# A convolution that builds each symmetric product once, with the MoE weights split a phase earlier and the last layer's first batch group taken batch by batch

## The chip, the cores and the metric

The kernel runs on one core of one Trainium2 chip. The metric is the device time of one execution in microseconds (us), inputs in HBM and output in HBM. The core's engines are TensorE (PE: matmuls, with PEld for its weight loads), VectorE (DVE), ScalarE (ACT), GpSimd (POOL) and SyncE (SP, which here only issues DMAs). Each has its own instruction stream; semaphores order them.

## What is computed

`x` is 16 batches x 128 tokens x 256 features. Four layers follow one another, each added to the residual `x`:

```python
# 1: gated long convolution. k = v = context, q = layernorm(x); 16 heads of 8 features
kv  = einsum('bhil,bhjl->bijhl', k, v)        # 8x8 products per head, channel and position
out = causal_conv(kv, ssm_kernel) + kv * D    # along l (256), by head
out = einsum('bijhl,bhil->bjhl', out, q)
# 2: MoE on layernorm(x): 16 routed experts (top 4 of the 2 best groups of 4) and a shared one
out = sum_e weight_e * (silu(x@gate_e) * (x@up_e)) @ down_e + swiglu(x, shared)
# 3: attention over features, per batch: softmax_d(q.T@k/16) applied to v = context
# 4: FFN of width 896 with LoRA experts, top 2 of 8 by softmax; silu(x1)*x3, twice
```

Here `l`, the 256 positions of the convolution, is the feature axis of `x`; the heads are cut from the token axis. Since `k = v`, `kv[i, j] = kv[j, i]`.

## The kernel before

`build` runs three phases one after the other: `first_phase` (convolution, the MoE's layernorm, router logits; 0 to 134.8 us), `moe_phase` (shared expert and routing to about 187, then the routed pairs to 351) and `tail_phase` (attention and the LoRA FFN). Each phase writes its engines' streams by hand; the order of the calls in each `@block` is the order on the engine. PE works in fp32 (two passes, shown as two matmul records) or, for the large products, in fp32r with each operand split in a high part `_hi` (a rounding copy) and a low part `_lo` (the rest) and three products, hi*hi, lo*hi and hi*lo.

**Convolution.** `CONV_ORDER` has 32 steps `(h, c)`: chunk `c` of 8 batches, head `h`. In step n POOL multiplies the 8x8 products of both halves of positions (L304, two instructions of 128x512) into one of 3 `kv` slots; PE multiplies them by the head's Toeplitz matrix (L408 to L410, three fp32 matmuls of 512 columns) into one of 2 pairs of PSUM banks; DVE multiplies by `q_t` (L545, twice 128x512) and sums over i (L554, twice) in place of `q_t`. From step 18 on, every third step also has one pair of tiles of the first chunk brought back: PE transposes it, DVE adds it to `x_sb` and takes statistics (`BACK_AT`, L501 to L514), POOL finds `rstd` (`RSTD_AT`, L251 to L257), ACT normalizes (L317), PE turns it, ACT copies it to `x_t` and casts to `x_hi` (L349, L352), POOL subtracts `x_lo` (L275). The second chunk's four pairs do the same behind the last step, with `x_lo` on DVE (L520).

**MoE weights.** 18 blocks of 128x768 are split. The first 8 go through a stage of 4 slots: ACT casts (L333), POOL subtracts (`weights_low(k)`, L269) at steps n = 2, 6, 10, ... ahead of the step's own products. The other 10 are split during the shared expert ("late"): ACT casts (L889) and writes the negative of the high part (L892), POOL adds the weight to it by an accumulating DMA (L962).

**Shared expert and routing.** 8 shared steps m. PE does gate and up (L583), ACT the silu (L872), DVE the product (`shared_product`, L1059), ACT the high part (L878), POOL the low part (L958), PE the down product (fp32r, `shared_down`); after each second step DVE adds two banks to `x_sb` (`add_to_x`, L1066, 2 x 128x512). Between these DVE finds the routing: top experts, ranks, slots, then one-hot tables for 4 blocks, `lane_hot` (L1101) and `tile_hot` (L1105, then times the token numbers, L1110), which PE turns into the list `slot_token` (L1119). POOL's gathers of the routed rows (L972) wait for that list. SP issues four loads of the last layer's weights (`lora_stage_early`, L723) when the table is done.

**Tail.** The routed rows are gathered back (L1657, 4 per batch). `attention_group` works on groups of 2 batches; group 0 runs alone ahead of the FFN: `add_routed` (L1755 to L1764), rstd on POOL (L605 to L609), `normalize` (L1772), scores on PE (L1459), `tops` (L1779), the exponentials on ACT (L1589), `scale_context` (L1786, L1793), `attention_out` (L1469), then the router (L1800 to L1853), the masks (L1610) and the first masked LoRA inputs `mix` (L1866), with which the FFN's steady work starts.

## Time and profile before

| | us |
|---|---|
| median of 3 runs | 859.78 |
| lowest, highest | 859.76, 860.88 |
| the profiled execution | 855.01 |
| its span | 853.3 |
| mean granted TensorE clock | 0.948 of full speed |
| busy: PE, DVE, POOL, ACT | 729.5, 549.2, 464.0, 328.3 |

The profile is of one execution. Its own time is 855.01 us, of which 853.3 lie between the first and the last instruction; it is 4.8 us under the median. A row of the timeline is one instruction, or a run of like ones: start, duration, engine, line, operation, output and inputs, count, and in brackets the idle time of the engine ahead of it with what ended that.

### The profile page before, as it was taken

To read this page: it belongs to the slowest core of one execution; us is meant where nothing else is said; L and a number is where in the kernel's file an instruction comes from. 1 tells how busy PE (TensorE), PEld (TensorE's weight loads), DVE (VectorE), ACT (ScalarE), POOL (GpSimd) and SP (SyncE) were. 2 spreads that over 40 slices of the span, in tenths; PEclk is the share of its full clock that TensorE was granted. 3 is DMA by queue.
4 is the path that set the end of the run, shared out by engine and by line. 5 is a ranking of instruction groups with operands and counts; after the bars stand their busy time and mean duration, and the time that the engine had idled before them with its cause. 6 is when DMAs were issued, how large, how long until landed. Compare 5 with 4: busy or idle time off the path is not lost.

```text
span 853.3 us, 14835 instructions
## 1 busy us (share of the span) xinstructions
PE 729.5 (85%) x5249; PEld 656.3 (77%) x5249; DVE 549.2 (64%) x1328; ACT 328.3 (38%) x680; POOL 464.0 (54%) x549
## 2 busy tenths in 40 slices
PE   4899989836778778238789999999999999999996
PEld 2344557736777778127789999999999999999996
DVE  4799977993445555348676767667666767654533
ACT  2221246612444445314454344444453343434321
POOL 4898963546455442336436636556475564543432
PEclk9899997967999999768899999999999999999999
DMA  8410014874555556342410201102011010000000
GB/s 257 152 38 12 26 37 122 186 157 160 147 152 144 139 146 123 106 139 77 127 35 25 65 1 57 32 13 63 13 32 57 1 50 27 1 14 1 2 13 13
DMA packets 42583, 63.16 MB, mean 74 GB/s; under 512 B 7152, under 2 KB 31760, under 8 KB 42512
## 3 DMA queue, kind: packets, MB, share of 16 engines
q1 hardware_dynamic: 34064, 38.71, 13.9%
q0 software_dynamic: 8352, 23.47, 12.3%
q8 instruction: 44, 0.72, 0.4%
q14 instruction: 27, 0.22, 0.1%
q10 hardware_dynamic: 96, 0.04, 0.0%
HBM read 47.37 MB, written 14.84 MB: 73 GB/s over the span
## 4 chain that ended last, share of the span: by engine, by line
PE 41%; DVE 6%; issue 4%; ACT 4%; POOL 3%; DMA 0%; POOLq 0%; ACTq 0%; DVEq 0%
PE bank L1387 15%; PE bank L1372 8%; PE bank L1419 6%; PE bank L1433 3%; PE bank L1405 3%; PE bank L1469 2%; DVE hid_lo L1883 2%; PE bank L1446 1%; ACT att_weights L1589 1%; POOL rows_back L1657 1%; DVE att_scaled L1793 1%; DVE am_lo L1872 1%; ACT am_hi L1574 1%; PE bank L1507 1%; ACT lora_w_hi L1550 1%
## 5 line engine op out<-in xcount | busy, mean ns | idle before, releaser
L1675 POOL TENSOR_TENSOR hid<-hid,rw_sb 128x256 f32<-128x256 f32 x112 | 90.7, 810 | 154.6 <-DVE hid L1877 154.4
L1387 PE MATMUL bank<-am_hi,lora_w_hi 128*128 128x256 f32 x448 | 126.9, 283 | 3.4 <-DVE am_lo L1872 3.4
L1877 DVE TENSOR_TENSOR hid<-hid,bank 128x256 f32<-128x256 f32 x112 | 46.7, 418 | 124.9 <-ACT hid L1557 124.2
L1387 PE MATMUL bank<-am_hi,lora_w_lo 128*128 128x256 f32 x448 | 126.7, 283 | 0.0
L1387 PE MATMUL bank<-am_lo,lora_w_hi 128*128 128x256 f32 x448 | 126.6, 283 | 0.0
L972 POOL DMA_INDIRECT rows_in<-y_scratch,slot_token x80 | 76.7, 958 | 76.5 <-DVE row_w L1173 44.6
L1557 ACT ACTIVATE hid<-bank 128x256 f32<-128x256 f32 x112 | 42.4, 385 | 183.3 <-PE bank L1387 170.7
L1387 PEld LDWEIGHTS bank<-am_hi,lora_w_hi 128*128 128x128 f32 x448 | 85.3, 190 | 3.6 <-POOL am_lo L1686 3.6
L1657 POOL DMA_INDIRECT rows_back<-slots_scratch,comb_idx x64 | 66.5, 1039 | 37.7 <-POOLq L666 22.2
L1387 PEld LDWEIGHTS bank<-am_hi,lora_w_lo 128*128 128x128 f32 x448 | 85.4, 191 | 0.0
L1387 PEld LDWEIGHTS bank<-am_lo,lora_w_hi 128*128 128x128 f32 x448 | 85.3, 190 | 0.0
L1883 DVE TENSOR_TENSOR hid_lo<-hid,hid_hi 128x256 fp32r<-128x256 f32 x112 | 71.2, 656 | 18.6 <-ACT hid_hi L1563 13.5
L1372 PE MATMUL bank<-lora_x_hi,lora_w_hi 128*128 128x256 f32 x224 | 67.8, 303 | 4.2 <-DVE lora_w_lo L1748 4.2
L304 POOL TENSOR_TENSOR kv<-ctx_t 128x512 f32<-128x512 f32 x64 | 64.7, 1042 | 2.8 <-PE bank L410 2.8
L1419 PE MATMUL bank<-hid_hi,lora_w_hi 128*128 128x256 f32 x224 | 62.9, 281 | 0.7 <-DVE hid_lo L1883 0.7
L1372 PE MATMUL bank<-lora_x_lo,lora_w_hi 128*128 128x256 f32 x224 | 63.2, 282 | 0.0
L1372 PE MATMUL bank<-lora_x_hi,lora_w_lo 128*128 128x256 f32 x224 | 63.1, 282 | 0.0
L1419 PE MATMUL bank<-hid_lo,lora_w_hi 128*128 128x256 f32 x224 | 62.6, 279 | 0.0
L1419 PE MATMUL bank<-hid_hi,lora_w_lo 128*128 128x256 f32 x224 | 62.5, 279 | 0.0
L1194 DVE SCALAR_TENSOR_TENSOR routed_h<-routed_silu,slot_w,bank 128x128 f32<-128x128 f32 x80 | 24.2, 344 | 50.2 <-issue 32.8
L545 DVE TENSOR_TENSOR prod<-bank,q_t 128x512 f32<-128x512 f32 x64 | 41.0, 682 | 17.4 <-PE bank L410 16.6
L848 PE MATMUL bank<-moe_w_hi,ht_hi 128*128 x80 | 24.4, 305 | 30.3 <-DVE ht_lo L1167 30.3
(259 smaller groups left out, 2245.6 us busy)
## 6 DMA issues: line engine op xcount, KB each, us to landing
slots_scratch<-y_out SPq DMA_DIRECT2D x40, 256.0 KB
lora_stage_early<-in_lora_weights SPq DMA_DIRECT2D x16, 384.0 KB, 3.2
...
```

The costliest lines, as they stand in the source:

```text
L304: last = nc.gpsimd.tensor_tensor(kv[:, n % KV_SLOTS, m, :].rearrange("p (b j i) -> p b j i", j=HEAD_DIM, i=HEAD_DIM), feat.unsqueeze(2).br ...
L545: nc.vector.tensor_tensor(prod[:, m, :].rearrange("p (b j i) -> p b j i", j=HEAD_DIM, i=HEAD_DIM), conv_banks[2 * (n % CONV_SETS) + m][:, ...
L972: nc.gpsimd.indirect_dma_start(out=rows_in[:, i % ROW_SLOTS, :], out_offset=None, in_=y_dram[:, :], in_offset=bass.IndirectOffsetOnAxis(ap ...
L1372: nc.tensor.matmul(x_banks[F % 2][:, w * GT:(w + 1) * GT], wp, xp, start=(w == 0 and c == 0 and k == 0), stop=False, skip_group_check=True)
L1387: last = nc.tensor.matmul(x_banks[F % 2][:, w * GT:(w + 1) * GT], wp, ap, start=False, stop=(half == 1 and k == 2), skip_group_check=True)
L1405: last = nc.tensor.matmul(a_banks[w][:, half * GT:(half + 1) * GT], wp, xp, start=(c == 0 and k == 0), stop=(c == HALVES - 1 and k == 2))
L1419: last = nc.tensor.matmul(term_banks[which][:, half * GT:(half + 1) * GT], wp, hp, start=(n == 0 and half == 0 and j == 0), stop=(n == FB ...
L1557: nc.scalar.activation(f[:, F % 2, k, :], x_banks[F % 2][:, 0:GT], ACT.Silu).then_inc(silu_done, 1)
L1657: nc.gpsimd.indirect_dma_start(out=rows_back[:, t % ROW_TILES, k * DIM:(k + 1) * DIM], out_offset=None, in_=slots_dram[:, :], in_offset=ba ...
L1675: nc.gpsimd.tensor_tensor(f[:, F % 2, k, :], f[:, F % 2, k, :], rw_sb[:, F // FB % 2, k, :], ALU.mult)\
L1877: nc.vector.tensor_tensor(f[:, F % 2, k, :], f[:, F % 2, k, :], x_banks[F % 2][:, GT:2 * GT], ALU.mult)\
L1883: nc.vector.tensor_tensor(hid_lo[:, F % 2, which, :], f[:, F % 2, 1 - which, :], hid_hi[:, F % 2, which, :].bitcast(FP32), ALU.subtract).t ...
```

## The change

- Convolution steps with odd n build 48 of the 64 products: 4x4 (low, low), which is enough for its quarter, and 8x4 (all, high); POOL has two instructions (128x16x16 and 128x16x32, these are 256 and 512 elements), PE 384 columns for each of the three matmuls, DVE three products (256, 256, 512 elements) and one sum of 1024. Even steps do all 64 with one instruction of 1024 on POOL and one product and one sum of 1024 on DVE. `prod` has one buffer for both.
- All 18 weight blocks are split in the first phase, by the method of the late ones: ACT casts and negates, POOL issues the accumulating DMA (`LOWS_AT`). There are 2 stage slots. The ACT order is new; `toeplitz(2)` is loaded ahead of the stage; row 3 of the queries is normalized on ACT.
- End of the first phase: `x_t` has 3 slots, and for the second chunk DVE does both the cast and the subtraction (`x_parts`).
- Shared down product from the unsplit fp32 rows: 4 fp32 matmuls per step, no high and low parts. `add_to_x` is replaced by two ACT copies (`shared_rows`) and a POOL accumulating DMA from SBUF to SBUF (`add_rows`), 4 times. The token-number products of blocks 0 to 2 are on ACT (`token_numbers`); `LANE_ORDER` is 0, 1, 2, 3.
- The four early LoRA loads stand one each ahead of the first four stores of routed rows.
- In the tail, group 0's chain is in the order of its batches: rstd, normalize, top, inverse, scale by batch, the gathers of batch 0 in one step and of batch 1 in the next two; `base(1)` follows `spread_picks`, and `mix` waits for its own mask only.

```diff
-SPLIT_EARLY = HEADS // 2
-STAGES, LATE_STAGES = 4, 2
+STAGES = 2
-LANE_ORDER = (0, 2, 1, 3)
+LANE_ORDER = (0, 1, 2, 3)
+HALF_HEAD = HEAD_DIM // 2
+OWN, KV_COLS = HALF_HEAD * HALF_HEAD, HALF_HEAD * (HALF_HEAD + HEAD_DIM)
+LOWS_AT = {5 + 2 * k if k < 3 else 11 + 5 * (k - 3) // 4: k for k in range(FBLOCKS)}
...
             def weights_low(k):
-                pool.wait_ge(hi_split, k + 1)
-                nc.gpsimd.tensor_tensor(w_lo[:, W_ORDER[k], :], stage[:, k % STAGES, :],
-                                        w_hi[:, W_ORDER[k], :].bitcast(FP32), ALU.subtract).then_inc(lo_split, 1)
+                pool.wait_ge(hi_split, 2 * k + 2)
+                nc.gpsimd.dma_start(w_lo[:, W_ORDER[k], :], a["moe_weights"][W_ORDER[k]], accum_op=ALU.add)\
+                  .then_inc(lo_split if k else first_low, 16)
...
-                if n % 4 == 2:
-                    weights_low(n // 4)
+                if n in LOWS_AT:
+                    weights_low(LOWS_AT[n])
...
+                low, high = feat[:, :, 0:HALF_HEAD], feat[:, :, HALF_HEAD:HEAD_DIM]
+                for first, rows, columns in (((0, low, low), (OWN, feat, high)) if distinct(n) else ((0, feat, feat),)):
...
             def weights_high(k):
                 act.wait_ge(staged[k % STAGES], 16 * (k // STAGES + 1))
                 nc.scalar.copy(w_hi[:, W_ORDER[k], :], stage[:, k % STAGES, :]).then_inc(hi_split, 1)
+                act.wait_ge(hi_split, 2 * k + 1)
+                nc.scalar.mul(w_lo[:, W_ORDER[k], :], w_hi[:, W_ORDER[k], :].bitcast(FP32), -1.0).then_inc(hi_split, 1)
...
+            query_copy(0)
+            query_rows(3)
+            for p in range(1, FIRST_HALF):
                 query_copy(p)
...
+            for k in range(3, FBLOCKS):
+                weights_high(k)
...
+                cols = slice(0, KV_COLS if distinct(n) else ALL_COLS)
...
+                if distinct(n):
+                    parts = ((low, low, out[:, :, 0:OWN].rearrange("p n (j i) -> p n j i", i=HALF_HEAD)),
+                             (low, high, out[:, :, OWN:2 * OWN].rearrange("p n (j i) -> p n j i", i=HALF_HEAD)),
+                             (high, everything, out[:, :, OWN:KV_COLS].rearrange("p n (i j) -> p n i j", j=HALF_HEAD)))
+                for j, i, y_ji in parts:
+                    shape = [P, width, j.stop - j.start, i.stop - i.start]
+                    last = nc.vector.tensor_tensor(prod[:, :, j, i], y_ji,
+                                                   query[:, :, i].unsqueeze(2).broadcast_to(shape), ALU.mult)
+                last.then_inc(prod_ready, 1)
...
-            def x_low(e):
+            def x_parts(e):
+                dve.wait_ge(xt_copied, e + 1)
+                x, hi, lo = x_t[:, e % X_SLOTS, :, :], token_cols(x_hi, 2 * P * e, 2 * P), token_cols(x_lo, 2 * P * e, 2 * P)
+                nc.vector.tensor_copy(hi, x).then_inc(hi_done, 1)
                 dve.wait_ge(hi_done, e + 1)
+                nc.vector.tensor_tensor(lo, x, hi.bitcast(FP32), ALU.subtract).then_inc(lo_done, 1)
...
-            for k in range(STAGE_SLOTS):
-                sp.dma_start(lora_stage[:, k, :], lora_unit(a, k)).then_inc(lora_staged, 16)
             for q in range(ROUTED_PAIRS):
                 sp.wait_ge(y_copied, q + 1)
+                if q < STAGE_SLOTS:
+                    sp.dma_start(lora_stage[:, q, :], lora_unit(a, q)).then_inc(lora_staged, 16)
...
                 for t in range(GROUP_T // P):
-                    rows = slice(t * P, (t + 1) * P)
-                    w = w_hi[:, n, 2 * DIM:3 * DIM], w_lo[:, n, 2 * DIM:3 * DIM]
...
+                    last = nc.tensor.matmul(out_banks[t // 2][:, (t % 2) * DIM:(t % 2 + 1) * DIM],
+                                            act[:, m % 2, t * P:(t + 1) * P], down_w[:, n, :],
+                                            start=(first and t % 2 == 0), stop=last_one, skip_group_check=True)
...
+            def shared_rows(g):
+                act_eng.wait_ge(down_done, SHARED_BLOCKS * (g + 1))
...
+                for o in range(2):
+                    nc.scalar.copy(shared_out[:, g % 2, 2 * o:2 * o + 2, :],
+                                   out_banks[o][:, :].rearrange("p (t d) -> p t d", t=2)).then_inc(out_copied, 1)
...
+            def add_rows(g):
+                pool.wait_ge(out_copied, 2 * (g + 1))
+                nc.gpsimd.dma_start(x_sb[:, 4 * g:4 * g + 4, :], shared_out[:, g % 2, :, :], accum_op=ALU.add)\
+                  .then_inc(x_added[g % 2], 16)
...
+            def token_numbers(block):
+                act_eng.wait_ge(tile_hit, block + 1)
+                for u in range(block * HOT_TILES, (block + 1) * HOT_TILES):
+                    rows = slice(u * TOP_EXPERTS, (u + 1) * TOP_EXPERTS)
+                    nc.scalar.activation(tile_hot[:, rows, :], tile_hot[:, rows, :], ACT.Copy,
+                                         scale=token_ids[:, u:u + 1]).then_inc(hot_ready, 1)
...
-            for t in range(TG):
-                add_routed(t)
+            add_routed(0)
+            normalize(0)
+            add_routed(1)
+            find_top(0)
+            normalize(1)
+            find_inverse(0)
+            scale_context(0)
+            find_top(1)
+            find_inverse(1)
+            scale_context(1)
```

The order of the instructions on POOL around step 2 of the convolution (`kv` are the products, `moe_w_lo` the low parts of the weights), before:

```order
L304 TENSOR_TENSOR kv<-ctx_t 128x512 x4
L269 TENSOR_TENSOR moe_w_lo<-early_stage,moe_w_hi 128x768
L304 TENSOR_TENSOR kv<-ctx_t 128x512 x8
L251 TENSOR_SCALAR rstd<-meanvar 128x4
L252 TENSOR_SCALAR shift<-meanvar 128x4
```

And after:

```order
L325 TENSOR_TENSOR kv<-ctx_t 128x1024
L325 TENSOR_TENSOR kv<-ctx_t 128x16x16
L325 TENSOR_TENSOR kv<-ctx_t 128x16x32
L325 TENSOR_TENSOR kv<-ctx_t 128x1024
L325 TENSOR_TENSOR kv<-ctx_t 128x16x16
L325 TENSOR_TENSOR kv<-ctx_t 128x16x32
L325 TENSOR_TENSOR kv<-ctx_t 128x1024
L290 DMA moe_w_lo<-in_moe_weights 128x768
```

The first low part of the weights moved from ahead of step 2 to ahead of step 5, and is a DMA.

On DVE at the end of the routing (`moe_act` is a shared product; `lane_hot` and `tile_hot` are the one-hot tables of a block; `reached` begins the tile table), before:

```order
L1101 TENSOR_TENSOR lane_hot<-lanes,lane_of 128x2048
L1059 TENSOR_TENSOR moe_act<-moe_silu,bank 128x512
L1066 TENSOR_TENSOR x_sb<-x_sb,bank 128x512 x2
L1105 TENSOR_TENSOR tile_hot<-tile_ids,tile_of 128x1280
L1110 TENSOR_SCALAR tile_hot<-tile_hot,token_ids 128x320 x4
L1101 TENSOR_TENSOR lane_hot<-lanes,lane_of 128x2048
L1105 TENSOR_TENSOR tile_hot<-tile_ids,tile_of 128x1280
L1110 TENSOR_SCALAR tile_hot<-tile_hot,token_ids 128x320 x4
L1101 TENSOR_TENSOR lane_hot<-lanes,lane_of 128x2048
```

And after:

```order
L1133 TENSOR_TENSOR lane_hot<-lanes,lane_of 128x2048
L1098 TENSOR_TENSOR moe_act<-moe_silu,psum 128x512
L1137 TENSOR_TENSOR tile_hot<-tile_ids,tile_of 128x1280 x2
L1133 TENSOR_TENSOR lane_hot<-lanes,lane_of 128x2048
L1137 TENSOR_TENSOR tile_hot<-tile_ids,tile_of 128x1280
L1144 TENSOR_SCALAR tile_hot<-tile_hot,token_ids 128x320 x4
L1133 TENSOR_TENSOR lane_hot<-lanes,lane_of 128x2048
```

The additions to `x_sb` and all but the last block's products with the token numbers left DVE's stream.

On DVE at the start of the tail (`rows_back` are the gathered rows of a batch), before:

```order
L1764 BN_AGGR meanvar<-stats 128x2
L1772 TENSOR_SCALAR att_y<-x_sb,meanvar,rstd 128x256 x2
L1779 TENSOR_REDUCE att_minus_top<-bank6 128x2
L1779 TENSOR_REDUCE att_minus_top<-bank7 128x2
L1786 RECIPROCAL att_inverse<-att_total 128x2 x2
L1793 TENSOR_SCALAR att_scaled<-ctx_ring,att_inverse 128x128 x4
```

And after:

```order
L1806 TENSOR_SCALAR att_y<-x_sb,meanvar,rstd 128x256
L1790 TENSOR_TENSOR rows_back<-rows_back 128x512
L1794 TENSOR_TENSOR x_sb<-x_sb,rows_back 128x256 x2
L1797 BN_STATS stats<-x_sb 128x6
L1799 BN_AGGR meanvar<-stats 128x2
L1811 TENSOR_REDUCE att_minus_top<-psum 128x2
L1806 TENSOR_SCALAR att_y<-x_sb,meanvar,rstd 128x256
L1816 RECIPROCAL att_inverse<-att_total 128x2
L1824 TENSOR_SCALAR att_scaled<-ctx_ring,att_inverse 128x128 x2
```

Batch 0's rows are normalized ahead of the addition of batch 1's routed rows, and its maximum, inverse and scaling stand beside batch 1's.

## Rows read from the trace of the kernel before

**Rows 1.** Timeline of DVE, steady convolution steps; start, duration, instruction, idle before
```profile
50.95 1.29 DVE L545 TENSOR_TENSOR prod<-bank,q_t 128x512 f32<-128x512 f32 x2 [0.98 <-PE bank L410]
53.52 1.29 DVE L545 TENSOR_TENSOR prod<-bank,q_t 128x512 f32<-128x512 f32 x2
...
77.76 1.25 DVE L545 TENSOR_TENSOR prod<-bank,q_t 128x512 f32<-128x512 f32 x2
...
80.12 1.28 DVE L545 TENSOR_TENSOR prod<-bank,q_t 128x512 f32<-128x512 f32 x2
```

**Rows 2.** Timeline of POOL, the wait ahead of step 2
```profile
21.10 1.81 POOL L269 TENSOR_TENSOR moe_w_lo<-early_stage,moe_w_hi 128x768 fp32r<-128x768 f32 x1 [6.00 <-ACT moe_w_hi L333]
```

**Rows 3.** Timeline of DVE, first product and the product behind the wait
```profile
18.93 1.29 DVE L545 TENSOR_TENSOR prod<-bank,q_t 128x512 f32<-128x512 f32 x2 [4.73 <-PE bank L410]
...
30.50 0.69 DVE L545 TENSOR_TENSOR prod<-bank,q_t 128x512 f32<-128x512 f32 x1 [4.99 <-PE bank L410]
```

**Rows 4.** Table by stretch: length; busy us of PE, PEld, DVE, ACT, POOL; clock, DMA share, GB/s
```profile
28.00:30.00 2.00, 2.00 (x3) 0.70 (x3) 0.00 (x0) 0.29 (x1) 0.89 (x1) 0.50 0.36 132
...
77.00:118.00 41.00, 38.35 (x133) 19.86 (x131) 36.03 (x71) 10.67 (x18) 35.51 (x43) 1.00 0.08 26
...
176.00:187.00 11.00, 5.10 (x60) 4.42 (x59) 10.93 (x16) 0.00 (x0) 0.86 (x1) 0.66 0.70 153
```

**Rows 5.** Timeline of DVE, short rows of 4, and the end of the routing
```profile
143.86 0.63 DVE L1024 TENSOR_TENSOR choice<-choice,g_mask 128x64 f32<-128x64 f32 x4
...
185.53 1.49 DVE L1116 TENSOR_TENSOR reached<-tile_nums,tile_end 128x1280 f32<-128x1280 f32 x1
187.06 0.24 DVE L1119 CAST slot_token<-bank 128x80 int32<-128x80 f32 x1
```

**Rows 6.** Timeline of DVE, a step with a pair brought back, and the last sums
```profile
73.94 0.68 DVE L501 TENSOR_TENSOR x_sb<-x_sb,bank 128x512 f32<-128x512 f32 x1
74.56 1.29 DVE L545 TENSOR_TENSOR prod<-bank,q_t 128x512 f32<-128x512 f32 x2
...
117.19 1.27 DVE L554 TENSOR_REDUCE q_t<-prod 128x64 f32<-128x512 f32 x2
```

**Rows 7.** Groups by line (busy us, mean ns, idle before), and all issues of L962 (ns, min/median/max)
```profile
L304 POOL TENSOR_TENSOR kv<-ctx_t 128x512 f32<-128x512 f32 x64 | 64.7, 1042 | 2.8 <-PE bank L410 2.8
...
L962 POOL DMA_DIRECT2D moe_w_lo<-in_moe_weights x10: 863/880/1142, 143.2 to 176.0; - x10
```

**Rows 8.** Timeline of ACT, a split by cast and negation; first normalized rows of the end
```profile
79.46 1.09 ACT L317 ACTIVATE y<-x_sb,shift,rstd 128x256 f32<-128x256 f32 x2 [17.96 <-POOL shift L257]
...
158.07 0.82 ACT L889 CAST moe_w_hi<-rows_in 128x768 fp32r<-128x768 f32 x1
158.91 0.85 ACT L892 ACTIVATE moe_w_lo<-moe_w_hi 128x768 fp32r<-128x768 f32 x1
```

**Rows 9.** Timeline of PE, the last logits of the first phase
```profile
131.02 3.43 PE L446 MATMUL bank<-moe_gate,moe_x_t 128*128 128x16 f32 x16
```

**Rows 10.** Timeline of DVE, routing tables beside the shared expert
```profile
167.70 0.94 DVE L1110 TENSOR_SCALAR tile_hot<-tile_hot,token_ids 128x320 f16<-128x320 f16 x4
...
171.36 1.28 DVE L1066 TENSOR_TENSOR x_sb<-x_sb,bank 128x512 f32<-128x512 f32 x2
172.55 2.93 DVE L1105 TENSOR_TENSOR tile_hot<-tile_ids,tile_of 128x1280 f16<-128x1280 f16 x1
...
178.58 1.48 DVE L1105 TENSOR_TENSOR tile_hot<-tile_ids,tile_of 128x1280 f16<-128x1280 f16 x1
```

**Rows 11.** Timeline of DVE: first rows of the routed loop, then group 0 in the tail
```profile
193.23 0.19 DVE L1173 TENSOR_TENSOR row_w<-rows_in,is_expert 128x32 f32<-128x32 f32 x1 [1.19 <-DMA rows_in<-y_scratch,slot_token]
...
364.30 0.69 DVE L1755 TENSOR_TENSOR rows_back<-rows_back 128x512 f32<-128x512 f32 x1 [2.72 <-DMA rows_back<-slots_scratch,comb_idx]
...
378.67 0.69 DVE L1800 TENSOR_TENSOR x_sb<-x_sb,bank 128x512 f32<-128x512 f32 x1 [3.68 <-PE bank L1469]
```

**Rows 12.** Table by stretch, start of the routed loop
```profile
192.00:197.00 5.00, 1.11 (x4) 0.71 (x4) 1.02 (x4) 0.58 (x1) 3.78 (x5) 0.50 0.96 366
```

359 lines of the change are left out of this document (172 added, 187 removed).

## The prediction

> **What bounds the kernel now.** I read the shares by engine first: TensorE (PE) is busy 729.5 of 853.3 us and carries the end of the chain. But the diff leaves the FFN's steady work and the routed loop as they are, so the question is which engine's wait ends last in each of the four places that it does touch. Those are read from the timelines.
>
> In the steady convolution the products on VectorE (DVE) start at 50.95, 53.52 and so on, 2.57 us apart, with an idle 0.98 in one of them that PE ends: PE is the bound, its three fp32 matmuls take 0.857 each. Where DVE has fallen behind it runs 2.36 per step [rows 1]. GpSimd (POOL) needs 2 x 1.04 = 2.1 [rows 7]. The three engines are nearly equal, so a gain on PE alone is small. One stop stands out: POOL waits 6.00 us ahead of step 2 for a high part of the weights [rows 2], DVE's product behind it comes 4.99 late [rows 3], and TensorE's granted clock is 0.50, its lower level of 1.2 GHz, while it recovers [rows 4]. From step 18 on no engine is full: in the 41 us from 77 to 118 PE is busy 38.35, DVE 36.03, POOL 35.51 [rows 4]; they wait for one another. While the routing is made DVE is the bound, busy 10.93 of 11.00 us before the list of slots at 187.06 [rows 4, 5]. The routed loop begins when the first gather lands, at 193.23, and the tail's start is a chain of group 0 through all engines [rows 11].
>
> **Convolution steps.** PE: even steps keep 3 x 0.857 = 2.57; odd ones have 384 of 512 columns, 1.93; mean 2.25, 0.32 less. POOL: an odd step has 768 elements instead of 1024, about 0.5 less than 2.1, if a row of 4 costs no more than its elements. DVE gets dearer: now product waits for sum and sum for product in one buffer. Rate: 1280 elements take 1.49 [rows 5], that is 0.15 + N/960; so 1024 take 1.22, with a gap of 0.03 twice 2.50 for an even step; an odd one 2 x 0.33 + 0.72 + 1.25 = 2.62, mean 2.56. That short rows are no dearer is read from four instructions with rows of 4 that take 0.63 together [rows 5]. So DVE replaces PE as the bound at 2.56, where it was 2.57: **the symmetric steps themselves give nothing in the first half** and take away what slack DVE had. Without any gain or with all of PE's they would be between 2.36 and 2.62.
>
> **The stop at step 2.** It goes, because nothing stands ahead of the products of steps 0 to 4. The first product was at 18.93 [rows 3] and is put at 18.0, since POOL's kv is not earlier but DVE has one row of queries less. Step 18's was at 74.56 [rows 6]. After: 18.0 + 18 x 2.56 + two rounds of statistics for queries that hid in the stop, 3.5, = 67.6. Gain 7.0. If conv steps take 2.62, 5.9; if the start stays, 0.9 less.
>
> **Steps 18 to 31.** Before, 74.56 to 118.46 (the sums at 117.19 take 1.27 [rows 6]), 43.9. DVE after: 14 x 2.56 plus four pairs brought back at 1.46 (73.94 to 77.76 is 3.82, less 2.36 [rows 1, 6]) = 41.7. POOL has here 3.5 less for products, and 9 issues of 0.88 [rows 7] in place of four subtractions of 1.81 [rows 2]: 0.7 more; busy about 33, no bound. Gain 1.9, between 0 and 3. Convolution together **8.9, range 6 to 10**.
>
> What the split adds to ScalarE (ACT): 18 units of 0.82 + 0.85 [rows 8] = 30.1 where 8 casts stood, in streams that were idle (17.96 ahead of its row at 79.46 [rows 8]). A pair of units is a cycle of about 5.2 with two stage slots (load 3.9 behind the first cast, by the page's median landing of such a load), so the 15 units behind the queries run from about 41 to 74 or 79. The first normalized rows are wanted at 76.5 then. A lateness of up to 3 us is possible and is partly caught by the pairs' spacing of three steps; I take 0, and 3 for the range.
>
> **End of the first phase.** From the last sum to the barrier it is a chain over four pairs. ACT's cast, 0.62 a pair, leaves it, the third slot of `x_t` takes the wait for logits away; DVE's extra cast is shorter than ACT's pace. PE's last logits took 3.43 at a low clock [rows 9] and stay. Four casts are 2.5, of which the last one was not on the path of the logits: gain **2, range 1.5 to 2.5**.
>
> **Routing.** What leaves DVE ahead of the slot list: three `add_to_x` at 1.20 (the row of 1.28 with its overlap) and three times four products with the token numbers at 0.86 (0.94) [rows 10], 6.2. And what POOL's subtractions did to DVE beside them: `tile_hot` took 2.93 where the same one took 1.48 [rows 10], another one 2.24; a few short ones of the top search went from 0.22 to 1.22 in the same way; in all 4.6, which go with the subtractions. That makes 10.8. The Trainium skill (SBUF — State Buffer, "SBUF: two separate sides") says that a DVE instruction with two SBUF inputs and a POOL one that reads SBUF lock each other out for the whole instruction; the row of 2.93 agrees, and without that rule the sum would be 6.2. PE is then the next late one: its fp32 down product is 4 matmuls of 0.43 = 1.7 instead of 12 of 0.117 = 1.4, and gate and up stay at 2.8 per step, at a clock that is low at first; two waits of DVE for it cost about 2.5 to 3.3. Gain at the list **7.5, range 6 to 10**: 179.6 instead of 187.06. Nothing of it waits on the list's path for the new copies on ACT (four times 1.1) or the additions by DMA, except that the last addition's DMA (512 KB, issued near 175) stands on POOL's queue ahead of the first gather: about 8 us from issue to landing, so until 183, as the gather lands 183 or later too. Cost 0, at most 2.
>
> **Start of the routed loop.** The first gather lands 5.65 after POOL's start at 187.58; DMA engines were busy 0.96 with 366 GB/s in 192 to 197 [rows 12], mostly the four LoRA loads of 384 KB. They now follow the first four pairs. Landing of a gather in the quiet tail takes 1.8 from its issue; here 3.2 and 4.4. Gain **2.5, range 1 to 3**. The loads are behind `y_copied`, needed first in the tail, 150 us later; SP queues only stores there, late by 0.1 each.
>
> **Tail start.** The chain before: batch 1's rows 364.30, att 378.67 [rows 11], then router and `mix` at 394.7. By batch, batch 0's normalization, scores (half of a cold 3.7) and exponentials stand in the wait for batch 1's rows; behind 364.3 there remain one batch's 2.1 of additions and statistics, rstd 1.4, one normalization, half the scores, one maximum, two exponentials, two scalings and half of `attention_out`: att at about 375.0, 3.7 earlier. A further 0.7 comes from the mask wait. Gain **4.4, range 3 to 5**. The FFN behind it is full on PE and moves with it.
>
> **Sum.** 8.9 + 2 + 7.5 + 2.5 + 4.4 = 25.3. The profiled execution of 855.01 becomes 829.7; it lies 4.8 under the median of the runs shown, 859.78, which I keep: **834.5**.
>
> **Rivals.** *First, ACT's weight chain is late.* If the accumulating DMA holds a slot longer or loads crowd with the second context load, the end rows come 3 to 6 us late and a part of the end chain with them: 834.5 + 4 = 838.5. For it: two slots instead of four; POOL waited for such a split 6.00 once [rows 2]. Against: ACT's 17.96 idle [rows 8].
> *Second, DVE is a bound that I priced too low*: extra gaps in odd steps, three dependent instructions, or slots that no longer overlap. At 2.8 per step, + 0.24 x 32 = 7.7, 842. It speaks for it that three engines lie within 15% [rows 1, 7].
> *Third, slower than before: rows of four are dear.* Place: the three DVE products of an odd step write and read 256 rows of 4 per partition. Each ns of a row's fixed cost is 0.256 us per odd step, 4.1 us in 16; it decides at 25.3/4.1 = 6.2 ns a row. At 10 ns the time is 875. Against it: 16 rows of 4 take 0.16 us [rows 5], 2 ns a row by the constants above.
> *Fourth, the change doesn't do what it says*: PE now idles in each step, and the granted clock falls to 1.2 GHz in the convolution, as it is 0.50 behind the stop and 0.66 at 176 to 187 [rows 4]. A step would take PE 4.5 instead of 2.56. That for half of the steps is + 31, 865. Against: at 38.35 busy of 41 it is 1.00 [rows 4].
> *Fifth, a better one*: the cover is looser and DVE reaches 2.45 per step, and all 10 of the routing: 834.5 - 3.5 - 2.5 = 828.5. The Trainium skill (same page and section) warns of the opposite, that DMA descriptors made by POOL wait while DVE holds the shared port in its fast modes; the longest of ten issues here was 1.14 against 0.88 [rows 7], so it would add at most 0.3 x 18 = 5 to a queue that has room.
>
> **How the numbers follow.** Forecast 0.52 (832 to 837), first rival 0.14, second 0.14, better one 0.12, slower one 0.03, clock 0.02 (865: slower too), no measurable change 0.03 by several of them together. Leaving out the last 0.08 and the far end of the others, the range is 827 to 843. The chance of faster by more than 0.2% (1.7 us, about what a measurement of this kernel can tell) is 0.93, same 0.02, slower 0.05.
>
> **What the profile of the changed kernel would show.** No wait of POOL over 1 us in the first 40 us, and clock 1.00 there; step 18 near 67.6; DVE steps of 2.50 and 2.62 in turn with PE waiting for DVE; last sum near 109.6, barrier near 124; slot list 44.9 behind the barrier (before 52.3); first routed row 3.5 behind the first gather's issue; tail's `mix` at 38 instead of 43.0 behind the loop's end. It would be wrong by a step that takes over 2.7, by ACT's units that end behind 80, or if the routing wait moved to PE and kept more than 4 us.

## The result: 1.5% faster, half of what was forecast

The changed kernel takes 848.12 us (median of 4 runs, 846.94 to 850.94), the kernel before 860.33 in the same job: ratio 0.9853, 95% interval 0.9823 to 0.9884, 12.2 us less. The forecast was 834.5 with a range of 827 to 843; the sign was right, the size and the range were wrong. The profiled execution of the changed kernel took 847.37, with a span of 845.6 and a mean granted clock of 0.945; it lies 7.6 under the profiled one of before. That one lay 4.8 under its median, this one 0.75.

Read by landmarks of the two profiles (start of a row; the last line is the last addition to `x_sb`):

| stretch | before | changed | difference | forecast |
|---|---|---|---|---|
| start to step 18's product | 74.56 | 71.21 | -3.4 | -7.0 |
| to the last sum's end | 43.9 | 51.6 | **+7.7** | -1.9 |
| to the router's scores | 16.3 | 16.5 | +0.2 | -2 |
| to the slot list | 52.3 | 45.8 | -6.5 | -7.5 |
| to the first routed row | 6.2 | 4.8 | -1.4 | -2.5 |
| routed loop, to the tail's first row | 158.4 | 162.2 | **+3.8** | 0 |
| tail to the first `mix` | 43.0 | 37.8 | -5.2 | -4.4 |
| to the last addition | 455.4 | 452.5 | **-2.9** | 0 |

The stop ahead of step 2 is gone, as forecast, and the steady steps of the convolution take 2.65 us on average: 2.58 from the start of an even step to the next one, 2.71 from an odd one. In this timeline of DVE of the changed kernel the columns are start, duration, instruction and the idle time before it, as in [rows 1]:

```profile
37.88 1.23 DVE L586 TENSOR_TENSOR prod<-psum,q_t 128x1024 f32<-128x1024 f32 x1
39.14 1.22 DVE L593 TENSOR_REDUCE q_t<-prod 128x128 f32<-128x1024 f32 x1
40.46 1.35 DVE L586 TENSOR_TENSOR prod<-psum,q_t 128x256 f32<-128x256 f32 x3
41.85 1.22 DVE L593 TENSOR_REDUCE q_t<-prod 128x128 f32<-128x1024 f32 x1
43.17 1.23 DVE L586 TENSOR_TENSOR prod<-psum,q_t 128x1024 f32<-128x1024 f32 x1
...
94.41 1.23 DVE L586 TENSOR_TENSOR prod<-psum,q_t 128x1024 f32<-128x1024 f32 x1 [11.12 <-PE psum L443]
```

The last row is the loss: a new stop of 11.12 us ahead of step 22. It is followed through the engines. PE, same kernel:

```profile
77.18 0.81 PE L443 MATMUL psum<-kv,toeplitz 128*128 128x384 f32 x2
89.36 1.11 PE L468 MATMUL psum<-ident,y 128*128 128x128 f32 x4 [11.38 <-ACT y L339]
90.27 1.91 PE L441 MATMUL psum<-kv,toeplitz 128*128 128x512 f32 x2
```

PE stands in front of the first turn of the end rows (`turn_rows(0)`, L468, in step 22 ahead of the step's own product) and waits for ACT's rows `y`; behind the wait its first product takes 1.91 instead of 1.02, at a granted clock of 0.50 (89.4 to 92 us), the lower level. ACT, same kernel, has the first of the 15 splits behind the queries, the last one and the rows:

```profile
43.58 0.84 ACT L355 CAST moe_w_hi<-stage 128x768 fp32r<-128x768 f32 x1
...
86.62 0.83 ACT L355 CAST moe_w_hi<-stage 128x768 fp32r<-128x768 f32 x1 [1.35 <-DMA stage<-in_moe_weights]
87.48 0.84 ACT L357 ACTIVATE moe_w_lo<-moe_w_hi 128x768 fp32r<-128x768 f32 x1
88.23 1.08 ACT L339 ACTIVATE y<-x_sb,shift,rstd 128x256 f32<-128x256 f32 x2
```

15 units from 43.58 to 88.32 are 2.98 each; the same row of before came at 79.46 [rows 8]. The reason for the length is in the idle brackets: ACT waits for the stage's load, 19.4 us in all of these 44.7. The page gives those loads 5.3 us to landing:

```profile
stage<-in_moe_weights SPq DMA_DIRECT2D x18, 384.0 KB, 5.3
moe_w_lo<-in_moe_weights POOLq DMA_DIRECT2D x18, 384.0 KB, 6.1
```

The theory I took to the chip: the end rows are queued behind 18 splits on ACT, PE meets their turn in order and stops, and that alone is most of what is missing. The rival: the splits' transfers and issues fill the second part anyway, and the wait only moves.

### The profile page after: what moved, and what is told of

Its sections match the earlier page's. It is cut to its first block, busy times and chain, and to the rows that moved or that the text cites. A ratio compares the mean times of both kernels' runs of the same rounds, so it can differ in the third digit from the quotient of the medians.

```text
span 845.6 us, 14731 instructions
## 1 busy us (share of the span) xinstructions
PE 725.4 (86%) x5217; PEld 660.0 (78%) x5217; DVE 542.3 (64%) x1278; ACT 339.8 (40%) x698; POOL 442.6 (52%) x532
## 4 chain that ended last, share of the span: by engine, by line
PE 48%; DVE 3%; POOL 3%; issue 2%; ACT 2%; POOLq 0%; DVEq 0%
PE psum L1417 18%; PE psum L1402 9%; PE psum L1449 8%; PE psum L1463 4%; PE psum L1435 3%; PE psum L1489 1%; PE psum L1476 1%; POOL rows_back L1688 1%; PE psum L1499 1%; PE psum L1537 1%; DVE lora_w_lo L1783 1%; PE psum L1517 1%; ACT lora_w_hi L1581 1%; PE psum L1507 0%; PE psum L1530 0%
## 5 line engine op out<-in xcount | busy, mean ns | idle before, releaser
L1417 PE MATMUL psum<-am_hi,lora_w_hi 128*128 128x256 f32 x448 | 128.0, 286 | 2.4 <-DVE am_lo L1903 2.1
L1417 PE MATMUL psum<-am_hi,lora_w_lo 128*128 128x256 f32 x448 | 127.8, 285 | 0.0
L1417 PE MATMUL psum<-am_lo,lora_w_hi 128*128 128x256 f32 x448 | 127.7, 285 | 0.0
L1417 PEld LDWEIGHTS psum<-am_hi,lora_w_hi 128*128 128x128 f32 x448 | 86.5, 193 | 3.0 <-POOL am_lo L1719 2.3
L1914 DVE TENSOR_TENSOR hid_lo<-hid,hid_hi 128x256 fp32r<-128x256 f32 x112 | 74.7, 688 | 19.4 <-ACT hid_hi L1594 14.5
L1417 PEld LDWEIGHTS psum<-am_lo,lora_w_hi 128*128 128x128 f32 x448 | 86.6, 193 | 0.0
L1417 PEld LDWEIGHTS psum<-am_hi,lora_w_lo 128*128 128x128 f32 x448 | 86.5, 193 | 0.0
L1402 PE MATMUL psum<-lora_x_hi,lora_w_hi 128*128 128x256 f32 x224 | 67.0, 299 | 6.1 <-DVE lora_w_lo L1783 6.1
L325 POOL TENSOR_TENSOR kv<-ctx_t 128x1024 f32<-128x1024 f32 (+2 forms) x48 | 64.6, 1517 | 5.1 <-PE psum L443 5.1
L1449 PE MATMUL psum<-hid_hi,lora_w_hi 128*128 128x256 f32 x224 | 62.9, 281 | 0.7 <-DVE hid_lo L1914 0.7
L1402 PE MATMUL psum<-lora_x_lo,lora_w_hi 128*128 128x256 f32 x224 | 62.6, 280 | 0.0
```

Source lines behind the costliest of these rows:

```text
L325: last = nc.gpsimd.tensor_tensor(kv[:, n % KV_SLOTS, :, first:first + shape[2] * shape[3]].rearrange("p n (i j) -> p n i j", j=shape[3]), ...
L1402: nc.tensor.matmul(x_banks[F % 2][:, w * GT:(w + 1) * GT], wp, xp, start=(w == 0 and c == 0 and k == 0), stop=False, skip_group_check=True)
L1417: last = nc.tensor.matmul(x_banks[F % 2][:, w * GT:(w + 1) * GT], wp, ap, start=False, stop=(half == 1 and k == 2), skip_group_check=True)
L1449: last = nc.tensor.matmul(term_banks[which][:, half * GT:(half + 1) * GT], wp, hp, start=(n == 0 and half == 0 and j == 0), stop=(n == FB ...
L1914: nc.vector.tensor_tensor(hid_lo[:, F % 2, which, :], f[:, F % 2, 1 - which, :], hid_hi[:, F % 2, which, :].bitcast(FP32), ALU.subtract).t ...
```

## Experiments

Four jobs of kernels (e, f, g, i), each timed beside the kernel before. Times of different jobs are compared through their ratios to it; "its partner" is the kernel that a run was edited from, e4_parts_behind_rstd for the runs f and g3. That kernel has 0.968 in job e and, repeated as i3, 0.971 in job i, so a difference of 0.003 between jobs is not told from none. Landmarks are of one profiled execution each.

| run | median us | ratio to before (95%) |
|---|---|---|
| e1_interleaved | 836.58 | 0.970 (0.965 to 0.976) |
| e2_no_stage_loads | 835.64 | 0.970 (0.966 to 0.974) |
| e3_no_symmetry | 840.43 | 0.975 (0.971 to 0.979) |
| e4_parts_behind_rstd | 835.52 | 0.968 (0.964 to 0.972) |
| f1_early_lora_loads | 837.01 | 0.971 (0.966 to 0.975) |
| f2_numbers_on_vector | 838.92 | 0.975 (0.971 to 0.978) |
| f3_group_by_pair | 837.06 | 0.973 (0.969 to 0.977) |
| f4_sum_in_halves | 834.85 | 0.971 (0.967 to 0.976) |
| g1_before_late_lora | 822.52 | 0.998 (0.996 to 1.000) |
| g2_before_new_tail | 812.89 | 0.988 (0.984 to 0.991) |
| g3_lows_two_later | 796.55 | 0.967 (0.964 to 0.971) |
| i1_changed_again | 846.76 | 0.983 (0.977 to 0.990) |
| i2_attention_by_group | 857.06 | 0.996 (0.993 to 0.999) |
| i3_repaired_again | 835.23 | 0.971 (0.965 to 0.977) |
| i4_both_repairs | 834.86 | 0.970 (0.965 to 0.976) |

### The order on ScalarE

```diff
-            for k in range(3, FBLOCKS):
+            for k in range(3, 14):
                 weights_high(k)
             for e in range(FIRST_HALF):
                 end_rows(e)
+                if 14 + 2 * e < FBLOCKS:
+                    weights_high(14 + 2 * e)
                 x_columns(e)
                 x_high(e)
+                if 15 + 2 * e < FBLOCKS:
+                    weights_high(15 + 2 * e)
```

> The changed kernel with one edit: on ScalarE the last four weight units stand between the first chunk's end rows instead of all ahead of them. My theory (end rows queued behind 18 splits stop TensorE at step 22, in order): TensorE's wait of 11.4 us ahead of the first turn of the end rows falls below 2, the last sum of the convolution comes at about 110 to 112 instead of 122.8, and the time falls from 848.1 by 10 to 12 us, to 836 to 838. Rival (the splits' DMAs or GpSimd's issues fill the second part, so that the wait only moves to GpSimd's low parts): the last sum stays behind 118 and the gain is under 4 us.

It measured 836.58, a ratio of 0.970 against 0.985 for the changed kernel. In the trace the last sum ends at 112.6 instead of 122.8, and this table of PE's waits from 70 to 115 us (in total, how often, longest) no longer has the end rows in it:

```profile
PE psum L445 <- POOL kv L325: 3.6, 4, 1.6
PE psum L460 <- DVE q_t L597: 2.1, 1, 2.1
PE psum L445 <- DVE prod L590: 0.2, 1, 0.2
```

ACT now has the rows at 75.28, between two splits:

```profile
74.37 0.84 ACT L357 ACTIVATE moe_w_lo<-moe_w_hi 128x768 fp32r<-128x768 f32 x1
75.28 1.09 ACT L339 ACTIVATE y<-x_sb,shift,rstd 128x256 f32<-128x256 f32 x2
78.92 0.83 ACT L355 CAST moe_w_hi<-stage 128x768 fp32r<-128x768 f32 x1 [2.54 <-DMA stage<-in_moe_weights]
```

So the splits had room in the second part, and the rival falls. The second run asks what makes the chain so long.

```diff
             for k in range(STAGES, FBLOCKS):
-                sp.wait_ge(hi_split, 2 * (k - STAGES) + 1)
-                load_stage(k)
+                pass
...
-                act.wait_ge(staged[k % STAGES], 16 * (k // STAGES + 1))
+                act.wait_ge(staged[k % STAGES], 16)
```

> The changed kernel without the stage loads of blocks 2 to 17: ScalarE splits what lies in the two slots, so the weights of the routed experts are wrong, and everything else is done. ScalarE's order is that of the changed kernel. If the chain of splits is bound by load and landing behind the two slots (2.98 us per unit measured, ScalarE's own part 1.67), it now ends near 70 instead of 88.3, the stop at step 22 vanishes and the time is 836 to 839. If ScalarE itself or its place behind the queries is the bound, the chain still ends behind 80 and at least half of the stop stays, 842 or more.

835.64. The edit also takes the traffic of these 16 loads away. With the order of the changed kernel, but nothing to wait for, the splits end at 67 and ACT then waits for GpSimd:

```profile
66.24 0.84 ACT L356 ACTIVATE moe_w_lo<-moe_w_hi 128x768 fp32r<-128x768 f32 x1
74.34 1.09 ACT L338 ACTIVATE y<-x_sb,shift,rstd 128x256 f32<-128x256 f32 x2 [7.26 <-POOL shift L277]
```

Either repair alone is enough: the stop is the product of a chain bound by its loads and of a queue order that put the urgent rows behind it. More stage slots, the plain remedy, were not tried.

### What the symmetric steps are worth

```diff
 def distinct(n):
-    return n % 2 == 1
+    return False
```

> As e1_interleaved, but all steps build all 64 products (one product and one sum of 1024 elements each on VectorE). My theory, that the symmetric steps give nothing because VectorE is the bound: an even step measured about 2.58 us, an odd one 2.71, so without symmetry TensorE takes over at 2.57 to 2.6 and the convolution is as long or up to 2 us shorter than in e1_interleaved. Rival (the 0.64 us less of TensorE and 0.5 of GpSimd per odd step is what makes room for the end work from step 18 on): 3 to 8 us longer than e1_interleaved.

840.43, 3.85 above its partner in the same job: the rival was nearer, at its lower end, though the two intervals overlap (0.971 to 0.979 and 0.965 to 0.976). Up to step 18 it is 1.1 behind (71.54 against 70.47, 0.85 of it already at the first product), from there 2.3 more (the sums end at 115.99 against 112.63). In these two traces 2.4 of the 3.4 are given back before the scores, 1.5 of them because the last logits ran at a clock of 1.00 here and of 0.50 there, as told below. So the symmetric steps are worth 3.4 us at the last sum, and what of it reaches the end isn't narrowed. With all products PE is busy 40.45 of the 42 us from 70 to 112; with 48 of them in odd steps it is busy 36.73 and DVE 39.26. These are the rows of e3_no_symmetry and of e1_interleaved in the table by stretch, columns as in [rows 4]:

```profile
70.00:112.00 42.00, 40.45 (x131) 20.14 (x130) 36.78 (x47) 19.34 (x29) 38.83 (x39) 1.00 0.68 154
```

```profile
70.00:112.00 42.00, 36.73 (x137) 20.63 (x136) 39.26 (x62) 20.19 (x30) 36.83 (x45) 1.00 0.65 145
```

From the first product to step 18 the two kernels are equal within 0.2 us (51.6 and 51.3), so there the symmetric steps give nothing, as forecast. From step 18 on the turns, transposes and logits share PE with the products and find room. My statement that symmetry gives nothing held for the first half alone.

### The end of the phase

```diff
+            dve.wait_ge(rstd_step, 3 * PAIRS_T)
             for e in range(FIRST_HALF, PAIRS_T):
                 x_parts(e)
```

> As e1_interleaved, and VectorE begins x_parts only when GpSimd has found all rstd of the end. In the changed kernel GpSimd's last four small instructions, beside VectorE's x_parts, took 2.5 us where their like took 1.4. My theory (the two lock each other out): the four take 1.4 again, the last end rows begin 1.1 us earlier, and the time is 0.5 to 1.5 us below e1_interleaved. Rival (the slowness is not from x_parts, or x_parts then are late themselves): no change or up to 1 us slower.

835.52 against 836.58, with intervals that overlap: the medians don't tell the two apart, the traces do. The changed kernel, GpSimd and VectorE at the last rstd:

```profile
130.30 0.32 POOL L272 TENSOR_SCALAR rstd<-meanvar 128x2 f32<-128x2 f32 x1 [0.18 <-DVE meanvar L547]
130.71 0.64 POOL L273 TENSOR_SCALAR shift<-meanvar 128x2 f32<-128x2 f32 x1
131.31 0.90 POOL L275 TENSOR_TENSOR rstd<-rstd,minus_half 128x2 f32<-128x2 f32 x1
132.29 0.66 POOL L278 TENSOR_TENSOR shift<-shift,rstd 128x2 f32<-128x2 f32 x1
```

```profile
130.13 0.41 DVE L553 CAST moe_x_hi<-moe_x_t 128x512 fp32r<-128x512 f32 x1
130.58 0.69 DVE L555 TENSOR_TENSOR moe_x_lo<-moe_x_t,moe_x_hi 128x512 fp32r<-128x512 f32 x1
131.75 0.43 DVE L553 CAST moe_x_hi<-moe_x_t 128x512 fp32r<-128x512 f32 x1 [0.48 <-ACT moe_x_t L373]
132.21 0.69 DVE L555 TENSOR_TENSOR moe_x_lo<-moe_x_t,moe_x_hi 128x512 fp32r<-128x512 f32 x1
```

And e4_parts_behind_rstd, the same four of GpSimd:

```profile
120.65 0.23 POOL L272 TENSOR_SCALAR rstd<-meanvar 128x2 f32<-128x2 f32 x1 [0.17 <-DVE meanvar L551]
120.96 0.22 POOL L273 TENSOR_SCALAR shift<-meanvar 128x2 f32<-128x2 f32 x1
121.13 0.71 POOL L275 TENSOR_TENSOR rstd<-rstd,minus_half 128x2 f32<-128x2 f32 x1
121.92 0.20 POOL L278 TENSOR_TENSOR shift<-shift,rstd 128x2 f32<-128x2 f32 x1
```

The four take 2.65 us from the first start to the last end in the changed kernel and 1.47 in e4_parts_behind_rstd. Each of the four slow ones ends 0.03 to 0.08 us behind the end of the VectorE instruction beside it: the 0.64 that began at 130.71 ends at 131.35, the subtraction at 131.27. The Trainium skill (SBUF — State Buffer, "SBUF: two separate sides") describes the shared port pair as held by one of the two for a whole instruction. These ends agree with it.

The stretch from the last sum to the scores is 16.7 in e1_interleaved and 14.2 here, but the lock is only half of that. The stretch ends with PE's last logits, sixteen matmul records. They begin 12.9 us behind the last sum in e1_interleaved and 11.6 here; in all six traces of changed kernels without the wait they begin at 12.0 to 12.9, in all eight with it at 11.2 to 11.7, before at 12.6. That difference, 1.1 us between the means, is what the wait gives. How long they then take follows the granted clock, 3.43 us at 0.50, 2.22 at 0.82 and 1.90 at 1.00:

```profile
135.57 3.43 PE L479 MATMUL psum<-moe_gate,moe_x_t 128*128 128x16 f32 x16
```

```profile
137.65 1.90 PE L479 MATMUL psum<-moe_gate,moe_x_t 128*128 128x16 f32 x16
```

The first row is of the changed kernel, the second of i1_changed_again, the same kernel in another execution, whose stretch is 14.3 without any repair. With the wait the stretch is 13.7 to 15.4 in eight traces. So the wait gives about 1 us, and the other 1.2 of e4's are the clock of that one execution.

### The routed loop and the LoRA loads

In every changed kernel of the first two jobs the loop took 161.0 to 163.9 us from the first row to the tail; before it took 158.4 in its one trace. ACT, changed kernel, among the first pairs:

```profile
199.77 0.58 ACT L948 CAST moe_xt_hi<-psum 128x512 fp32r<-128x512 f32 x1 [2.48 <-remote]
205.49 0.38 ACT L961 ACTIVATE routed_silu<-psum 128x256 f32<-128x256 f32 x1 [5.13 <-remote]
```

The matmuls of the second row's silu are done by the records at 199.4; "remote" is a releaser that the trace has no record of. Is it the moved loads?

```diff
+            for k in range(STAGE_SLOTS):
+                sp.dma_start(lora_stage[:, k, :], lora_unit(a, k)).then_inc(lora_staged, 16)
             for q in range(ROUTED_PAIRS):
                 sp.wait_ge(y_copied, q + 1)
-                if q < STAGE_SLOTS:
-                    sp.dma_start(lora_stage[:, q, :], lora_unit(a, q)).then_inc(lora_staged, 16)
```

> As e4_parts_behind_rstd (835.5 us), with the four LoRA loads back ahead of the routed loop. In the four kernels with the loads in the loop, the stretch from the first routed row to the tail takes 162.0 to 163.7 us, before it took 158.4, and the stretch from slot list to first row 4.8 instead of 6.2. If the moved loads cause the longer loop, it is 158.5 to 160 here and the time is 1 to 3 us lower; the first row lands 6 us behind the list again. If they do not (something else holds ScalarE at the third pair, for 5.1 us), the loop stays at 162 or more and the time is 1 to 2 us higher.

837.01. The first row lands 5.9 behind the list again and the fourth pair comes 19.7 behind it, as before (21.9 in its partner), but from first row to tail it is 162.0, unchanged, and the same hold of 5.13 us is there, one silu earlier. Not the loads. The opposite edit, alone on the kernel before:

> The kernel before with only the four LoRA loads moved behind the first routed pairs. In the profile of before the first routed row came 6.2 us behind the slot list and the fourth pair 19.7 behind it. My forecast gave this move 2.5 us. If the fourth pair is held by something else (in all changed kernels ScalarE stands still for about 5.1 us once among the first pairs, and the fourth pair comes 19.7 to 21.9 behind the list whenever the first row landed), the first row comes at 4.8 but the fourth pair not before 19.5, and the time is within 1 us of before. If the move pays, the fourth pair comes at 17 to 18 and the time is 2 to 3 us lower.

822.52 to 824.39, ratio 0.998 (0.9963 to 0.9997). In this job the kernel before took 824 us instead of 860, for a reason that isn't known. It has no trace of its own there; in the trace of g1_before_late_lora the 40 pairs take 112.9 us from the first to the last, 2.89 each, where the trace of before has 146.4 and 3.75. These 33.5 us are nearly all of the difference. The loop has no wait of ACT for "remote":

```profile
230.68 0.38 ACT L919 ACTIVATE routed_silu<-bank 128x256 f32<-128x256 f32 x1 [0.34 <-PE bank L825]
231.61 0.37 ACT L898 CAST ht_hi<-bank 128x256 fp32r<-128x256 f32 x1 [0.55 <-PE bank L834]
232.05 0.59 ACT L906 CAST moe_act_hi<-bank 128x512 fp32r<-128x512 f32 x1
232.53 0.59 ACT L912 COPY y_out<-bank 128x512 f32<-128x512 f32 x1
233.47 0.39 ACT L919 ACTIVATE routed_silu<-bank 128x256 f32<-128x256 f32 x1 [0.34 <-PE bank L825]
```

The fourth pair came 14.3 behind the list, less than both cases of the expectation; with the loads ahead of the loop, in g2_before_new_tail of the same job, it came 17.9 behind. In this job the loads' price is 1.9 us by the medians, at most 3 by the interval.

### The tail

```diff
             add_routed(0)
-            normalize(0)
             add_routed(1)
-            find_top(0)
+            normalize(0)
             normalize(1)
-            find_inverse(0)
-            scale_context(0)
+            find_top(0)
             find_top(1)
+            find_inverse(0)
             find_inverse(1)
+            scale_context(0)
             scale_context(1)
```

> As e4_parts_behind_rstd, with VectorE's order of group 0 in the tail back to both batches at each stage. From the tail's first instruction to the first mix it is 37.8 to 38.9 us now, 43.0 before. If that order is what the tail gained by, it is 41 to 43 here and the time 3 to 5 us higher. Rival (the masks and the moved base product are what counts): under 40 and less than 2 us higher.

837.06, ratio 0.973 against 0.968 and 0.971, which doesn't tell it from its partner. The trace has 39.7 us to the first mix against 38.8: the order on VectorE alone is worth about 1, and the rival holds. The whole tail on the kernel before:

> The kernel before with the whole tail of the changed one. In the changed kernel the tail, from its first instruction to the last addition, is 8.1 us shorter than before, 5.2 of it ahead of the first mix. If the tail's edit makes all of it, the time is 6 to 8 us under before; if only the start is its doing, 4 to 5.

812.89, 11.5 under before by the medians; the ratio, 0.988 (0.984 to 0.991), allows 7 to 13, so it is above the lower case and perhaps above the upper. By landmarks, against the trace of g1_before_late_lora in the same job, 5.2 of it is ahead of the first mix and 6.1 behind it, in the FFN's steady work that I had called unchanged. The rows that show it are PE's waits from first mix to the end, kernel before and changed kernel:

```profile
PE bank L1469 <- DVE att_scaled L1793: 7.9, 7, 4.2
PE bank L1372 <- DVE lora_w_lo L1748: 4.2, 4, 1.2
```

```profile
PE psum L1402 <- DVE lora_w_lo L1783: 6.1, 5, 1.4
PE psum L1499 <- DVE att_scaled L1824: 3.6, 1, 3.6
```

The attention product waited 7 times, 7.9 us in all, now once for 3.6; the waits for `lora_w_lo` grew from 4.2 to 6.1. The last job takes that one edit back out of the changed kernel:

```diff
-                for k in range(TG):
-                    pe.wait_ge(exp_done, HALVES * (TG * G + k + 1))
-                    pe.wait_ge(scaled_done, HALVES * (TG * G + k + 1))
+                pe.wait_ge(exp_done, HALVES * TG * (G + 1))
+                pe.wait_ge(scaled_done, HALVES * TG * (G + 1))
+                for k in range(TG):
```

> The changed kernel, where TensorE's attention product again waits for both batches of its group before it begins. In the kernel before, that product waited for VectorE's scaled context in 7 of 8 groups, 7.9 to 8.7 us in all, 4.2 to 5.0 of it once; in the changed kernel once behind group 0, 3.6. If these waits by batch are the part of the tail's gain that I missed, six or seven groups lose 0.7 each again: the stretch from the first mix to the end grows by 3 to 5 us, and the time is 4 to 6 us above i1_changed_again. Rival (the moved weight units and the mask's wait did it): under 1.5 us.

857.06 against 846.76 for the changed kernel beside it: 10.3 us, of the 13.6 that the whole change gained in that job. The waits are back:

```profile
PE psum L1499 <- DVE att_scaled L1824: 8.1, 7, 4.4
```

By landmarks it is 1.7 ahead of the first mix and 4.4 behind it, 6.1 of the 6.9 that the two profiled executions differ by. The profiled execution of i1_changed_again took 851.14, 4.4 above its median (its routing has a wait of 2.52 for TensorE that no other trace has), so the traces can't place the rest of the 10.3. The wait of `attention_out`, which the diff changes for all eight groups, carries most of the tail's gain; its size is 6 by the traces and 10 by the medians, and I can't narrow it.

### VectorE and GpSimd in the repaired kernel

```diff
-            for block in range(HOT_BLOCKS - 1):
-                token_numbers(block)
```

(with the products back on VectorE for all blocks)

> As e4_parts_behind_rstd, with the products of the one-hot tables with the token numbers of blocks 0 to 2 back on VectorE. From scores to slot list the changed kernels take 45.8 us. If VectorE bounds that stretch alone, three groups of four at 0.86 come on top: 48.4, and the time is 2.6 us higher. If TensorE's shared steps bound it (4.46 us between two of them, VectorE waits of 0.5, 1.6 and 0.2 for it), part of it hides: 46.5 to 47.5, 1 to 2 us higher.

838.92, ratio 0.975 against 0.968 and 0.971. From scores to list it is 48.5 against 45.8, 2.7: VectorE bounds that stretch, and the sum's price of 0.86 a group was right. Two edits to its partner for the convolution:

> As e4_parts_behind_rstd, with VectorE's sum in two halves of 512 in each step and the product of an even step in two halves, so that an instruction seldom waits for the one right before it. If the waits between product and sum (spacing 1.26 and 1.33 of instructions of 1.22) are what makes VectorE the bound of the steps, a pair of steps takes 4.9 to 5.1 instead of 5.30, the last sum comes 3 to 5 us earlier and the time is 831 to 833. Rival (the extra instructions cost as much as the waits, or GpSimd is the next bound at once): within 1 us of e4_parts_behind_rstd.

834.85, ratio 0.971: no gain, the rival. Its last sum comes at 115.2, no earlier than the 114.8 of f1_early_lora_loads in the same job, whose convolution is the partner's. The instructions did get denser, but from step 7 on VectorE waits 0.34 for TensorE in each pair of steps, and two steps take 5.4. This timeline of TensorE in f4_sum_in_halves shows why:

```profile
42.83 1.02 PE L447 MATMUL psum<-kv,toeplitz 128*128 128x512 f32 x2
43.69 1.04 PE L428 MATMUL psum<-ident,y 128*128 128x128 f32 x8
44.56 0.81 PE L445 MATMUL psum<-kv,toeplitz 128*128 128x384 f32 x2
...
49.87 0.91 PE L445 MATMUL psum<-kv,toeplitz 128*128 128x384 f32 x2 [0.64 <-POOL kv L325]
```

TensorE is busy without a gap over steps 7 to 10 (10.70 of 10.70 us from 38.5 on): the products of two steps, 4.50, and the turns of the queries, 0.87, are 5.37. Behind them it waits for GpSimd's products. Where VectorE stops being the bound, TensorE or GpSimd is the next at once.

```diff
-LOWS_AT = {5 + 2 * k if k < 3 else 11 + 5 * (k - 3) // 4: k for k in range(FBLOCKS)}
+LOWS_AT = {5 + 2 * k if k < 3 else 13 + 5 * (k - 3) // 4: k for k in range(FBLOCKS)}
```

> As e4_parts_behind_rstd, with GpSimd's issues of the low parts from the fourth on two convolution steps later. There GpSimd waits 7.6 us for ScalarE's negated parts, 4 times, with the products of the next step queued behind; TensorE waited for products 6.2 us in e1_interleaved. If this wait is on the path, the last sum comes 1.5 to 4 us earlier (109 to 111) and the time is 832 to 834. Rival (three slots of products cover it): within 1 us of e4_parts_behind_rstd.

Ratio 0.967 (0.964 to 0.971), as e4's 0.968; the last sum ends at 111.2 against 112.7, and GpSimd waits 3.9 us for ScalarE's negated parts instead of 7.6. Small, as the rival says. Both together, beside the changed kernel and the repaired one:

> The changed kernel itself, beside the kernel before on the same chip. If the routed loop is again held (over 155 us from first row to tail), the gain is about 12 us as measured. If the loop runs free (112 us), the 3.8 us that it had grown by are not lost: the gain is 15 to 17 us, ratio 0.980 to 0.983. The stop of about 11 us at step 22 is there in either case, ending at 89 us.

> Same kernel as e4_parts_behind_rstd, beside i1_changed_again on the same chip. The two edits take away the stop at step 22 and the contention at the end of the phase: 12 to 15 us under i1_changed_again, whatever state the routed loop is in.

> As i3_repaired_again, with the sums in halves and the low parts two steps later. Each alone gave about 1 us or less. If the two stood in each other's way (VectorE's waits for TensorE came with GpSimd's waits for ScalarE), together they give 3 us or more; if VectorE's own work is the bound, at most 1.5 us.

846.76, 835.23 and 834.86. The changed kernel has 0.983 where it had 0.985, inside both intervals, and its stop again, of 12.64 us here; the repair is 11.5 faster, just under the expectation; the two finer edits add nothing that can be told. The best kernel of the study is the changed one with its ACT order interleaved and `x_parts` behind the rstd: ratio 0.968 to 0.971 to before, 25 us.

## Why the prediction was wrong

**The term that failed** is that of ACT's chain: "the 15 units behind the queries run from about 41 to 74 or 79 ... I take 0, and 3 for the range". Three things in it were off. The sum was not done: 15 units at half of 5.2 from 41 is 80, not 79 or less. The unit was too short, 2.98 instead of 2.6, since I took the median landing of 3.9 from the loads of the shared expert, where the DMA engines were 0.90 busy at 193 GB/s; here, from 44 to 81, they are 0.96 busy at 229 GB/s, and the landing is 5.3. That this traffic makes the difference is not tested by itself. The page of before also had 7.5 for the first phase's own stage loads, which I passed over. The start was 43.6. Together that ends at 88.3. Then the price, which was the larger error: I let the pairs' spacing catch the lateness, but PE is in order and the first wait stands ahead of a product of the convolution. Of the wait of 11.4, 9.4 show in the stretch from step 18 to the last sum (51.6 against 42.2 in e1_interleaved), with a clock of 0.50 behind it. The first rival named this case and gave it 4 us and 0.14; its mechanism was the right one, its size was 10 to 12.

Taking that away, e1_interleaved, e4_parts_behind_rstd and i3_repaired_again give 835 to 837, which is the forecast of 834.5 within about 2 us. That closeness is luck in good part. The forecast for a profiled execution was 829.7, and e4's took 835.5, 5.8 more; the 4.8 that I added as the offset of before to its median did not appear in e4, which lies at its median. By terms:

- **The stop at step 2**: gone as forecast. Step 18 came at 71.2, in the repaired kernels 69.1 to 73.2, not 67.6. The step costs 2.65, not 2.56 (0.10 between a sum and the next product where I put 0.03): 1.6. The first product came at 19.2 instead of 18.0, and PE waited for products behind POOL's waits for ACT.
- **Steps 18 to 31**: 42.2 us in e1_interleaved, forecast 41.7. Right, once the stop was out. (The sum I wrote gives 43.9 - 41.7 = 2.2, where I entered a gain of 1.9.)
- **End of the phase**: forecast -2, measured +0.2. The last logits begin 0.2 later than before; with the wait of e4 they begin 0.9 to 1.4 earlier, so the lock between VectorE and GpSimd took about 1 of the 2. The rest was never there, or hides in the logits' own 1.90 to 3.43 by clock, which I had as a fixed 3.43. I had cited that rule for the routing and not applied it where the change puts new two-input work of VectorE beside GpSimd's.
- **Routing**: forecast 44.8 behind the scores, measured 45.8. VectorE's waits for TensorE were 4.1 (0.69, 1.19, 0.52, 1.55, 0.18), about 1 more than taken.
- **First rows**: the first came 4.3 behind the gather's issue, forecast 3.5, and 4.8 behind the list where it had been 6.2; but the fourth pair came at 21.7 where it had been 19.7. The gain was lost at once, with ACT's hold in the loop beside it, which no row of before that I showed tells of.
- **Tail**: forecast -4.4, measured -8.1, in g2 -11.4 by its trace. The first part was near (-5.2). The step that failed is "the FFN behind it is full on PE and moves with it": the diff changes `attention_out` for all eight groups, and the trace of before had the wait that it removes, 7 times.

Faster, given 0.93, came true. The second rival (a dearer VectorE step) was true by a third of its size. The third falls: the three products of an odd step take 1.35, under the 1.38 of the forecast. It was also miscounted: the edit has 128 rows of four, in the products of 256 elements, and the third product has 64 rows of eight, not 256 rows of four in all. The fourth falls too: in the convolution the clock was 1.00 but for the stop and the steps behind it. Each of the three signs of being wrong that I named came: ACT's units ended at 88.3, an odd step took 2.71, and VectorE's wait for TensorE in the routing was 4.1; only the first was dear.

**What stays open.** What holds ACT for 2 to 5 us at a silu in the routed loop, why that is absent in one job, whose loop is 33.5 us shorter, and so whether the changed kernels' longer loop (3.8) is a cost of the change; of before only one such trace exists. In the job without holds the loop of g3_lows_two_later took 112.1 us from first to last pair, against 112.9 in g1 and in g2, no loss. That speaks against a cost of the change itself, but the changed kernel did not run there. In that job the kernels with the routing of before also took 55.5 us from scores to list, where before had 52.3, while g3_lows_two_later had 45.8, as in the other jobs; why is open too.
